# First stage of a language-model tower: latents and rotary keys from rounded-32-bit parts, and a new order of statistics, gathers and remainders

## What is computed

```python
h = table[x]                                   # 8192 rows of 256
n = layernorm(h)
lat_q, lat_kv = n @ Wd_q + b, n @ Wd_kv + b    # 128 columns each
query = lat_q @ Wu_q + b + rope(lat_q @ Wq_r + b)
key   = lat_kv @ Wu_k + b + rope(n @ Wk_r + b)
value = lat_kv @ Wu_v + b_v
h = h + softmax(query @ key.T / scale) @ value @ Wo + b_o   # 16 heads of 16, per batch row
h = h + mixture_of_experts(layernorm(h))       # 32 experts, top 1, capacity 320
```

## Time and profile before

| | us |
|---|---|
| median of 3 runs | 3316.14 (3315.4 to 3316.4) |
| profiled execution | 3315.87 |
| its span, first to last instruction | 3314.0 |
| busy: PE, DVE, ACT, POOL | 3202.7, 2908.6, 2468.7, 565.3 |
| end of the first stage (DVE's last `full`) | 284.1 |
| attention | to about 2917 |
| routing, experts | to about 3061, to 3314.0 |

### The profile page before, as it was taken

The page is one execution under the profiler, slowest core; times in us unless marked ns, Lnnn a source line. Parts: engine busy times, 40 slices in busy tenths (PEclk is TensorE's granted clock), DMA queues, the critical chain, the costliest instruction groups (busy, mean ns, idle before and its releaser), DMA issues.

```text
span 3314.0 us, 67613 instructions
## 1 busy us (share of the span) xinstructions
PE 3202.7 (97%) x27520; PEld 1369.7 (41%) x27520; DVE 2908.6 (88%) x3157; ACT 2468.7 (74%) x4578; POOL 565.3 (17%) x752
## 2 busy tenths in 40 slices
PE   7997999999999999999999999999999999986999
PEld 3443333333333333333333333333333333365666
DVE  6889999999999999999999999999999999567222
ACT  3331888888888888888888888888888888943221
POOL 7882000000000000000000000000000000046233
PEclk9997999999999999999999999999999999998999
DMA  6895213131313131313131313122222220168773
GB/s 201 256 299 159 54 49 72 37 72 37 72 38 72 38 74 38 72 40 72 37 72 39 83 34 79 39 70 44 65 45 58 45 83 21 37 204 305 231 238 101
DMA packets 269155, 305.40 MB, mean 92 GB/s; under 512 B 45270, under 2 KB 198399, under 8 KB 265517
## 3 DMA queue, kind: packets, MB, share of 16 engines
q1 hardware_dynamic: 256812, 271.63, 29.7%
q0 software_dynamic: 12032, 29.45, 2.7%
HBM read 165.81 MB, written 139.23 MB: 92 GB/s over the span
## 4 chain that ended last, share of the span: by engine, by line
PE 81%; ACT 4%; DVE 3%; issue 2%; POOL 1%; DMA 0%; another core or an unknown queue 0%; SPq 0%; POOLq 0%; DVEq 0%
PE ps_o L916 33%; PE ps_s L899 26%; PE ps_m L868 13%; ACT probs L1012 2%; PE ps_g L1592 2%; PE ps_y L1603 2%; PE ps_u L1592 2%; DVE max_parts L1027 2%; ACT weighted L992 1%; PE ps_td L1581 1%; ACT rows_c L1343 1%; POOL slot_rows L1257 0%; PE ps_s L883 0%; POOL shift_c L1234 0%; DVE stats_c L1377 0%
## 5 line engine op out<-in xcount | busy, mean ns | idle before, releaser
L1027 DVE TENSOR_REDUCE max_parts<-ps_m 128x2 f32<-128x1024 f32 x2048 | 2486.1, 1223 | 79.9 <-PE ps_m L868 71.5
L1012 ACT ACTIVATE probs<-ps_s 128x512 f32<-128x512 f32 x4096 | 2217.5, 597 | 312.3 <-PE ps_s L899 127.8
L868 PE MATMUL ps_m<-keys,queries 48*128 48x512 f32 x4096 | 1483.5, 453 | 17.1 <-DVE max_parts L1027 16.7
L899 PE MATMUL ps_s<-queries,keys 51*128 51x512 f32 x4096 | 1480.5, 447 | 9.5 <-ACT probs L1012 3.1
L916 PE MATMUL ps_o<-probs,vals 128*32 128x256 f32 x16384 | 1295.5, 391 | 0.0
L899 PEld LDWEIGHTS ps_s<-queries,keys 51*128 51x128 f32 x4096 | 610.5, 185 | 832.2 <-issue 785.2
L868 PEld LDWEIGHTS ps_m<-keys,queries 48*128 48x128 f32 x4096 | 595.4, 187 | 77.4 <-DVE max_parts L1027 50.2
L916 PEld LDWEIGHTS ps_o<-probs,vals 128*32 128x32 f32 x16384 | 329.4, 108 | 720.4 <-issue 699.0
L824 POOL TENSOR_TENSOR heads_out<-weighted,recip_rows 128x512 f32<-128x512 f32 x63 | 80.9, 1285 | 2147.4 <-DMA recip_rows<-recip_rows_dram 2147.4
L1663 DVE TENSOR_TENSOR hidden<-ps_u,silu 128x320 f32<-128x320 f32 x64 | 31.5, 492 | 127.4 <-PE ps_u L1592 101.6
L1639 ACT ACTIVATE silu<-ps_g 128x320 f32<-128x320 f32 x64 | 28.0, 438 | 134.1 <-PE ps_g L1592 82.8
(11 more groups left out here) (108 smaller groups left out, 1600.0 us busy)
## 6 DMA issues: line engine op xcount, KB each, us to landing
slot_rows<-empty SPq DMA_DIRECT2D x16, 1290.0 KB, 5.2
vext<-val SPq DMA_DIRECT2D x64, 256.0 KB
halves_q<-parts SPq DMA_DIRECT2D x64, 256.0 KB
halves_k<-parts SPq DMA_DIRECT2D x64, 256.0 KB
keys<-halves_k SPq DMA_DIRECT2D x32, 512.0 KB, 7.5
queries<-halves_q SPq DMA_DIRECT2D x128, 128.0 KB, 3.2
vals<-vext SPq DMA_DIRECT2D x32, 512.0 KB, 5.6
recip_rows<-recip_rows_dram SPq DMA_DIRECT2D x64, 256.0 KB
```

The costliest lines, as they stand in the source:

```text
L868: mm = pe.matmul(ps_m[m % 2][:, h, :], queries_r[par][rows, qt, p, t * P:(t + 1) * P], keys_r[par][rows, p, c * 512:(c + 1) * 512], start= ...
L899: pe.matmul(ps_s[bank][:], keys_r[par][rows, p, k * P:(k + 1) * P], queries_r[par][rows, qt, p, :], start=True, stop=True).then_inc(scores ...
L1012: act.activation(probs[:, n % RING, :], ps_s[bank][:], ACT.Exp, scale=SCALE).then_inc(probs_ok[bank], 1)
L1027: dve.tensor_reduce(max_parts[:, lu % 2, :, p, t, c], ps_m[m % 2][:], AX.X, ALU.max).then_inc(maxima_ok[m % 2], 1)
```

## The change

Numbered as the prediction takes them.

1. The latents and the rotary keys are no longer fp32 products. The weights are split once, at the start, in a rounded part and a remainder (four DVE instructions), and the normalised, transposed rows in every chunk: ACT writes the high part (in place of `normed_t`), DVE the low part (`low_rows`, new). Each fp32 product becomes three products of the rounded 32-bit type: high x high, remainder of the weights x high, weights x low. So 12 matmuls for the latents, 12 for the keys.
2. The keys' rotary terms: two of the four are written back into PSUM, so that each of DVE's two sums of the keys reads one operand from PSUM and one from SBUF.
3. The values' bias is not added in the first stage. ACT copies the values (in place of DVE's addition), and in the attention POOL adds the bias to the normalised result, one more instruction of 128x512 per unit, 64 in all. Its column is loaded by four DMAs with 4-byte elements before the attention.
4. The statistics run three chunks ahead and stand behind the keys' sums on DVE; moments and the two inputs of `root` (minus mean, variance plus epsilon; before on POOL) run on DVE two chunks ahead, ahead of the queries' `add_content`. The third stage gets the same inputs of `root` on DVE, and its moments ahead of `gate`.
5. On PE the transposes stand ahead of the queries' content part.
6. POOL's list for chunk n becomes: the waits of the gather; gather(n+3); `sums` of the queries; `root(n+2)`, now two instructions; remainder of the keys of chunk n-1; remainder of the queries of chunk n. ACT's high part of the keys moves to chunk n+1 likewise.

SP's list of a chunk is not changed.

```diff
@@ phase_a, gpsimd: chunk
                     pool.wait_ge(norm_ok, b * (CPB * CT) + k * CT)
                     pool.wait_ge(emb_out[ahead[1]], ahead[0] * 16)
                     pool.wait_ge(ids_in[ahead[1]], ahead[0] * 16 + 16)
+                    gather(*ahead)
 
                 pool.wait_ge(terms_ok[0], after(b, k, 4))
                 pool.wait_ge(full_ok[0], b * (CPB * 2) + k * 2)
                 pool.tensor_tensor(sums[:, 0, 0, :], terms[:, 0, 0, :], terms[:, 0, 1, :], ALU.subtract).then_inc(sums_ok[0], 1)
                 pool.tensor_tensor(sums[:, 0, 1, :], terms[:, 0, 2, :], terms[:, 0, 3, :], ALU.add).then_inc(sums_ok[0], 1)
-                if ahead:
-                    gather(*ahead)
-                for x in range(2):
-                    if x == 1 and not (last and k + 2 >= CPB):
-                        root(*((b, k + 2) if k + 2 < CPB else (b + 1, k + 2 - CPB)))
-
-                    pool.wait_ge(high_ok[x], after(b, k))
-                    pool.tensor_tensor(parts[:, k % 2, x, 1].bitcast(F32R), full[:, x], parts[:, k % 2, x, 0], ALU.subtract).then_inc(low_ok[x], 1)
+                if not (last and k + 2 >= CPB):
+                    root(*((b, k + 2) if k + 2 < CPB else (b + 1, k + 2 - CPB)))
+                if (b, k) != (0, 0):
+                    rest(*((b, k - 1) if k else (b - 1, CPB - 1)), 1)
+                rest(b, k, 0)
@@ phase_a, tensor: latent
                 for x in range(2):
                     for d in range(KD):
-                        last = pe.matmul(ps_l[:, x, :], w_down[:, x, d, :], normed_t[:, k % 2, d, :],
-                                         start=d == 0, stop=d == KD - 1)
+                        for p in range(2):
+                            pe.matmul(ps_l[:, x, :], w_down_r[:, p, x, d, :], high_r[:, k % 2, d, :],
+                                      start=d == 0 and p == 0, stop=False, skip_group_check=True)
+                pe.wait_ge(nt_low_ok, after(b, k))
+                for x in range(2):
+                    for d in range(KD):
+                        last = pe.matmul(ps_l[:, x, :], w_down_r[:, 0, x, d, :], low_r[:, k % 2, d, :],
+                                         start=False, stop=d == KD - 1, skip_group_check=True)
                     last.then_inc(lat_ps, 1)
@@ phase_a, vector
+            def key_sums(b, k):
+                dve.wait_ge(terms_ok[1], after(b, k, 4))
+                dve.tensor_tensor(sums[:, 1, 0, :], terms_k[:, 0, :], ps_r[:, 1, :], ALU.subtract).then_inc(sums_ok[1], 1)
+                dve.tensor_tensor(sums[:, 1, 1, :], terms_k[:, 1, :], ps_r[:, 0, :], ALU.add).then_inc(sums_ok[1], 1)
+            def low_rows(b, k):
+                dve.wait_ge(nt_ok, after(b, k))
+                dve.tensor_tensor(low_r[:, k % 2], ps_t[:], normed_h[:, k % 2], ALU.subtract).then_inc(nt_low_ok, 1)
@@ phase_a, vector: chunk
                 rope_terms(b, k, 0)
-                dve.wait_ge(val_out[k % 2], uses(b, k, CT * 16))
-                ...  # two additions of the values' bias
+                if not (last and k == CPB - 1):
+                    low_rows(*((b, k + 1) if k + 1 < CPB else (b + 1, 0)))
+                ...
+                    row_moments(*ahead)
+                    root_inputs(*ahead)
                 add_content(b, k, 0)
-                ...
                 rope_terms(b, k, 1)
-                ...
+                key_sums(b, k)
+                if third:
+                    row_stats(*third)
                 add_content(b, k, 1)
@@ phase_a, scalar: chunk
                 if more:
                     copy_nt(*nxt)
+                if (b, k) != (0, 0):
+                    split(*((b, k - 1) if k else (b - 1, CPB - 1)), 1)
+                copy_val(b, k)
                 split(b, k, 0)
                 if more:
                     copy_lat(*nxt)
-                split(b, k, 1)
```

More of the change, by code:

```diff
@@ L472, in chunk @@
                 rotary(b, k, 0)
+                early = more and (b, k) != (0, 0)
+                if early:
+                    transpose(*nxt)
                 content(b, k, 0)
                 values(b, k)
-                if more:
+                if more and not early:
                     transpose(*nxt)
@@ L493, in copy_nt, with copy_val @@
                 act.wait_ge(trans_ok, after(b, k))
-                act.activation(normed_t[:, k % 2], ps_t[:], ACT.Copy).then_inc(nt_ok, 1)
+                act.activation(high_r[:, k % 2], ps_t[:], ACT.Copy).then_inc(nt_ok, 1)
+            def copy_val(b, k):
+                act.wait_ge(val_out[k % 2], uses(b, k, CT * 16))
+                for h in range(2):
+                    act.wait_ge(val_ps, after(b, k, 2) - (1 - h))
+                    act.activation(val[:, k % 2, 2 * h:2 * h + 2, :, 0:HD],
+                                   ps_l[:, h, :].rearrange("p (t h d) -> p t h d", t=2, d=HD), ACT.Copy).then_inc(val_ok, 1)
             def copy_lat(b, k):
@@ L538, in _ @@
                 chunk(BATCH - 1, k, True)
+            split(BATCH - 1, CPB - 1, 1)
         @block.vector
@@ L589, in chunk @@
                 add_content(b, k, 0)
-                ahead = None if last and k + 2 >= CPB else (b, k + 2) if k + 2 < CPB else (b + 1, k + 2 - CPB)
-                if ahead:
-                    row_stats(*ahead)
-                    dve.wait_ge(stats_raw, after(*ahead, CT))
                 rope_terms(b, k, 1)
-                if ahead:
-                    row_moments(*ahead)
-                dve.wait_ge(terms_ok[1], after(b, k, 4))
-                dve.tensor_tensor(sums[:, 1, 0, :], terms[:, 1, 0, :], terms[:, 1, 1, :], ALU.subtract).then_inc(sums_ok[1], 1)
@@ L599, in chunk @@
-                dve.tensor_tensor(sums[:, 1, 1, :], terms[:, 1, 2, :], terms[:, 1, 3, :], ALU.add).then_inc(sums_ok[1], 1)
+                key_sums(b, k)
+                third = None if last and k + 3 >= CPB else (b, k + 3) if k + 3 < CPB else (b + 1, k + 3 - CPB)
+                if third:
+                    row_stats(*third)
                 add_content(b, k, 1)
-            bv_twice = b_v[:].rearrange("p (a h d) -> p a h d", a=1, d=HD).to_broadcast([P, 2, HEADS, HD])
             for b in range(BATCH - 1):
```

182 lines of the change are left out of this document (106 added, 76 removed).

## The result

The changed kernel takes 3361.82 us (median of 4 runs, 3358.27 to 3370.21), the kernel before 3316.27 us beside it (3315.4 to 3317.53). The ratio is 1.014, 95% interval 1.0127 to 1.0152: 1.4% slower. The forecast was 3343.5 us, its own range 3335 to 3358, the wide one 3326 to 3370. The profiled execution took 3361.44 us, its span 3359.5 us, 45.5 us more than before.

A forecast was written before the change was run, and what follows sets the result against it. The second loop, through SP's list and POOL, bounds the first stage: 34.5 + 252.3 + 8.7 + 6.6 + 9.6 = 311.7 us, +27.6 on 3315.87, the rest 0: 3343.5 us. Own range 3335 to 3358, wide range 3326 to 3370.

The forecast's parts named there:

- second loop: First stage: keys' remainder, SP's list, embedding store's landing, gather, sums and root bind chunks at 18.0 us; forecast's chance 0.72.
- rival (b): PE's clock in the first stage falls to 1.2 GHz in the gaps; at half the time, 3360 us; chance 0.13.
- Rival (c): Rounded products on PE take 0.43 us each, so 18.2 us per first-stage chunk and 3361 us; chance 0.02.
- The turn: One round of the second loop in the first stage: 18.0 us, ends 17.5 and 19.0; eleven make 198.0.
- The loads in the loop: Attention's loads in SP's list ahead of the embedding store: keys' +8.7 us (4.6 to 12.9), queries' +2.2 each, 6.6 together.
- Start: First stage: POOL, free at 29.5 us, gathers first, so the first sums start at 34.5 instead of 33.18.
- first interval: First stage, chunk 0 to 1: 13.7 us plus 0.7 for two sets of statistics under POOL's sums, 14.4.
- last intervals: First stage, intervals to chunks 13, 14 and 15: 13.7 us, then PE's 13.1 each, 39.9 in all.
- end: From the sums of chunk 15 to the end of the first stage: 9.6 us.
- Attention: POOL's 64 more instructions, about 1.3 us each, cost 0; the bias column's DMAs 0, bounds 0 and +2 us.
- Third stage: Two tiny DVE instructions, +3 us, against moments that fill a wait, -3: 0, bounds -4 and +4.
- Rival (a): First stage: second loop doesn't bind, a loop through DVE and POOL sets 13.7 us per chunk; 3284 us, chance 0.13.

The follow-up runs named there:

- Experiment 1: Changed kernel, but SP issues chunk n's token numbers and embedding store ahead of the keys' parts of chunk n-1: 3299.96 us, ratio to before 0.9954.
- experiment 4: Kernel before, with only the new order on POOL and ACT (gather ahead of sums, keys' remainder and high part a chunk later): 3444.0 us, ratio 1.039.
- Experiment 2: Changed kernel, with POOL's gather moved back behind the sums of the queries: 3327.59 us, ratio to before 1.0037.
- experiment 3: Changed kernel, with latents and rotary keys as fp32 products again: 3360.3 us, ratio to before 1.0137.
- Experiment 5: Experiment 1, with SP issuing the attention's loads only behind the next chunk's embedding store and keys' parts: 3305.93 us, ratio to before 0.9978.
- experiment 7: Experiment 1, with latents and rotary keys as fp32 products again: 3305.4 us, ratio to before 0.9969.
- experiment 11: Kernel before, with one unused tile of 16 bytes per partition ahead of the attention's second set of keys: 3318.56 us, ratio 1.0007.
- experiment 8: Experiment 1, with all four rotary terms of the keys in SBUF, as before the change: 3316.8 us, ratio to before 1.0001.

## Why the prediction was right and where its size was off

**The bound and the loop: right.** The forecast said that the second loop, through SP's list, would set the time. POOL waits before the gather in eleven chunks, 5.33 us in the one shown (3 to 5 taken), DVE waits 6.21 us for the sums, the last two intervals take 13.4 us, the eleven of the loop 18.5 to 19.3 where no load stands in them. Experiment 1 opens the loop by SP's list alone and the 18.6 us are gone; experiment 4 closes it in the kernel before. Experiment 2 agrees but has a second limit at the same length.

**The size: 17.9 us too low, and held by the wide range alone.** 3361.4 us lies above the forecast's own range of 3335 to 3358. The range to 3370 takes it in because it was widened for rival (b), PE's clock, which cost nothing in the turns (experiment 3). That the rivals (b) and (c) were priced at 3360 and 3361 us is a coincidence too. Of the excess 9.6 us are in the first stage, 4.5 in the attention, 2.5 and 1.2 behind it.

**The turn: 18.56 us for 18.0.** By steps, from the rows shown: remainder and SP woken 2.38 (taken 2.4); first issue to embedding store 3.12 (3.13); store issued to gather 4.50 (3.57, which is 6.6 + 0.1 less 3.13); gather 4.80 (4.8); sums 2.47 (2.6); root 1.29 (1.5). The one that was mis-sized stands between the store's issue and the gather. Its landing, from the trace (DMA issues, 150.6 to 151 us: count, KB, us from issue to landing):

```profile
emb_rows<-emb SPq DMA_DIRECT2D x1, 512.0 KB, 3.7
```

So the store landed 6.86 us after the first issue, close to the 6.6 taken. What was missing is the step behind it: from the landing at 154.44 to the gather at 155.20 it takes 0.76 us where 0.1 was taken, and 0.75 to 0.77 in each of the eleven waits. 0.27 and 0.66 us are the difference; 11 turns make 6.2 us with the small steps. What the 0.76 us consist of was not tested. (The 5.6 us that the prediction sets beside its 6.6 was worked out for DMAs that POOL issues; SP issues this store.)

**The loads in the loop.** The keys' load made one interval 30.5 us, so +11.9 where +8.7 stood as the middle of 4.6 and 12.9. It was nearly the upper end, which was the row of the same load in the kernel before; the lower end was a rate without anything alongside. The row should have been taken. Each load of queries cost 2.2, 2.2 and 1.9 us (2.2 taken). Experiment 5 shows why the keys' load has its price wherever it stands.

**Start, first interval, last intervals, end.** The first sums start at 34.0 (34.5), the first interval is 13.7 (14.4), the last three 40.5 (39.9), the end 9.5 (9.6). All terms of the first stage together: 321.3 against 311.7. The 9.6 are 6.2 + 3.2 of the two terms above, and 0.2 net of small ones, among them 1.2 us of turns longer than the one shown.

**Attention, taken as 0: +4.5.** The term was mis-sized, and not for the reason that was weighed (more work on POOL): POOL's 64 additions (101.3 us in all, 1.58 each) cost nothing that shows. 40.49 us per unit with padding and without a bias is as long as the changed kernel's 40.48 with it. It was the placement of the tiles, which the prediction didn't think of.

**Third stage, taken as 0 within 4: +2.5; fourth +1.2.** In the chain after, three loads of the third stage stand that the chain before doesn't have (start us, us, what):

```profile
2984.34 13.74 DMA att_t<-att
...
3003.41 11.20 DMA att_t<-att
3020.77 12.16 DMA att_t<-att
```

Over all kernels run here this stage took 150.7 to 157.4 us, and the last one 245.5 to 247.1, without an order that follows the edits. Inside the third stage one step of the working holds: a chunk took 7.4 and 8.6 us by turns before, and 7.6 or 7.7 in most chunks after. Around the three loads four chunks of the kernel after took 8.3, 8.9, 12.8 and 8.6 us, which uses up that gain and more. Why the loads take so long there was not looked for.

**Rival (a), the open loop.** It named the right mechanism for experiment 1: 13.7 us per chunk from DVE's list. The DVE list came out at 13.45 where the sum gave 13.7. The rest was too good. With the loop opened the first stage ends at 265.2 us, not 252.6, because the keys' load still costs a wait of 11 us and the queries' loads 2 us each. 298 GB/s stood against the 308 worked out.

**Rival (b), PE's clock.** It fell, and it did not matter. The clock after is 0.94 from 60 to 140 us, 0.90 from 30 to 321 us, and goes to its lower level in stretches such as 185 to 199 us, where PE is busy 4.28 of 14 us at 0.52. Experiment 3, with longer products, has the same turn, so PE's slack covers it.

**Rival (c), the price of a rounded product.** 0.235 us where 0.21 to 0.23 was taken from the earlier trace rows. Experiments 3 and 7 put its worth at nothing in the turns with the loop closed (2.9 us in the whole stage) and 5.1 us with it open.

## What to carry to other kernels

When work is moved later in one engine's list and something else earlier, follow the queue that serves both: here SP's list tied the gather of chunk n+3 to the remainder of chunk n-2 by a store that stood behind it, and moving that store up was worth 62 us, more than the rounded products, the terms in PSUM and the moved bias together (5.1, 15.8 and 5.0 us with the loop open). A part of a change that shows no gain may be hidden by such a loop; test it again with the loop open before dropping it. Between two bounds for a transfer, take the row measured under the same load, not one measured alone.

## What the runs showed of the hardware

- An unused tile of 16 bytes per partition, ahead of the attention's second set of keys, makes a unit of the attention 40.49 us instead of 40.41, 5 us in 2600 (experiment 11). Which of the tiles behind it matters wasn't tried.
- From the landing of a store to the first gather on POOL that waits for it the changed kernel took 0.75 to 0.77 us in eleven waits. A store of 512 KB with four of 256 KB issued ahead of it landed 3.7 us after its issue, where such stores took 3.0 in the attention.
- A DVE instruction of 128x4 elements in SBUF, 0.17 us by itself, took 1.32 us beside one of POOL's sums and ended with it (experiment 1). A DVE sum with both operands in SBUF took 2.57 us beside POOL's remainder (experiment 8), with one in PSUM 0.69. By the Trainium skill, "SBUF — State Buffer", section "SBUF: two separate sides", DVE and POOL lock each other out for a whole instruction where DVE has two SBUF inputs and POOL reads SBUF, or where DVE works in a two-port mode; the sums agree with the first, 2.57 against 0.69 us. That the small instruction, which has one input, works in such a mode is not shown by any trace; its 1.32 against 0.17 us would fit.
- Writing a 128x512 result of the rotary terms to PSUM took DVE 0.75 us, to SBUF 0.74 (experiment 1).
- A product of rounded 32-bit parts is one instruction and starts 0.235 us behind the last (after, granted clock 1.0), against 0.86 us for an fp32 product of the same size, so three of them cost 0.71.
